# Cosformer attention and a two-of-eight expert layer in one kernel: attention in sub-chunks of 64 tokens, every attention product in four 64x64 tiles of TensorE's array

## The chip, the cores and the metric

The kernel runs on one core of one Trainium2 chip. The metric is the time of one execution on the device in microseconds (us). TensorE (PE) multiplies matrices, VectorE (DVE), ScalarE (ACT) and GpSimd (POOL) work elementwise, SyncE (SP) issues DMAs. Matrix products land in PSUM, in the program the array `ps` of eight banks of 512 floats on 128 partitions; everything else lies in SBUF. A matmul holds one operand in the array (LDWEIGHTS loads it) and streams the other through. Every matmul that the program writes on 32-bit floats appears in the trace as two loads and two matmuls; transposes, and matmuls of the type F32R, appear as one.

## What is computed

`x` has 2,048 tokens of 128 features. The first half is attention with 16 heads of 64 features on the normalised tokens (weights and biases as arrays):

```python
Q, K, V = (xn @ Wq + bq), (xn @ Wk + bk), (xn @ Wv + bv)      # 16 heads of 64
Qp, Kp = relu(Q), relu(K)
# at each token t, with cos_t and sin_t of the angle pi/(2T) * t:
S_cos += (Kp*cos_t) outer V;  S_sin += (Kp*sin_t) outer V     # 64x64 per head
z_cos += Kp*cos_t;            z_sin += Kp*sin_t
num = (Qp*cos_t) @ S_cos + (Qp*sin_t) @ S_sin
den = max(sum(Qp*cos_t*z_cos + Qp*sin_t*z_sin), 1e-6)
x = x + concat_heads(num / den) @ Wo + bo
```

The state runs over all tokens, so the attention is causal. The second half normalises again, picks the best 2 of 8 experts for each token, and adds `gelu(x @ w1 + b1) @ w2 + b2` of both, weighted by the softmax of their two scores.

## The kernel before

**Stages.** The tokens go through four stages `i` of 512 (NS = 4), each of four chunks `c` of 128 (SC = 4). A stage has a *front* (projections to qT, kT, kn and vcs, with the tail of the stage before between them) and an *attention* part. After the last stage come 39 expert blocks of 128 rows (`hidden`, `down`), which read rows that were scattered to `ybuf` by expert.

**A chunk of attention.** Queries and keys lie transposed in qT and kT (a head on 64 partitions, two heads to a slot), keys also by token in kn, and values times cos and times sin, with a column for z, in vcs (65 columns each, VW). The denominator needs no separate product: it is that column. The work of a stage is 16 groups `n` of four heads (four groups to a chunk), taken in 8 pairs `p`:

- `scores` (L1135): keys by queries for eight heads, 128x128 each, into banks 0 and 1. VectorE multiplies them by `pair` (1 + tan tan, causal) into `am` (`masked`, L751).
- `before` (L1152): queries by the state up to this chunk, 130 columns (cos and sin side by side), 64 partitions deep.
- `within` (L1173): `am` by the chunk's values, 65 columns, added to the cos half in PSUM, and then keys by values (L1180), 130 columns, into a third region of the same banks: what the chunk adds to the state.
- ScalarE copies the sine half out (`out_sums`, L598), VectorE adds the third region to `state` (L761) and joins the halves, cos + tan * sin, into `tcs` (L767). Banks 2 to 5 are two pairs that the groups take in turn.
- Once a chunk, VectorE makes the reciprocals (L771, L774), GpSimd scales (`normalise`, L432, into `on`, which has two buffers), TensorE turns the result in eight transposes (`turn_out`, L1200), ScalarE copies it to `oT` (L553), and TensorE projects it (`project`, L1209). VectorE adds the projection to `x_sb` (`residual`, L779).

**Sizes and tiles of the array.** L1135 and L1152 run as two matmuls at a time in two halves of the rows (64x128), L1173 and L1180 in two halves of the columns (128x64), all others in the whole array.

**Order.** Each engine's instructions stand in an order written out by hand, with a wait on a semaphore wherever one engine needs another. TensorE's order in attention is, for p = 1 to 8: scores(p), outputs(p-1), then a turn or a projection. Beside that, in stages 1 to 3, VectorE ranks the tokens of the stage before (`places` L854 to L864, after masked(1)), ScalarE takes the tanh for their shares (`share`, after group 1), VectorE writes the shares (`shares` L845, after groups 0 and 1), and GpSimd sends the rows to `ybuf` in eight scattered DMAs (`rows_paced`, L474), spread over the stage by the groups that are done. GpSimd also adds the bias bo (`open_residual`, L440) and normalises the next stage's x (L446). SP may load the first two expert blocks only when the last of stage 2's rows has landed (L384, L377), and TensorE turns both (L1259) at the end of attention 3, in `first_rows`.

Of the kernel before, what the change touches and what calls it, by code (L numbers as in the profile page):

```python
# [28 lines left out]
P = 128  # L29
# [12 lines left out]
CS = 2 * VW  # L42
GH = 4
# [8 lines left out]
PH = 2 * GH  # L52
PAIRS = GROUPS // 2
# [6 lines left out]
OT_AT, WO_AT, YT_AT, GATE_AT = 3, 5, 11, 14  # L60

# [30 lines left out]

def z_bank(b):

    return 7 if b >= Z_TWO and b % 2 else 4
# [5 lines left out]
def moe_block(nc, x, Wq, bq, Wk, bk, Wv, bv, Wo, bo, gate_w, w1, b1, w2, b2,  # L101
              c_rot, c_pair, c_ident, c_small, c_tri, c_ids, out, ybuf, zbuf):
    with ExitStack() as ctx:
# [19 lines left out]
        pair = sb("pair", [P, SC, P])  # L123
# [5 lines left out]
        blank = sb("blank", [P, BR, ROW])  # L129
# [10 lines left out]
        am = sb("am", [P, 2, 2, PH // 2, P])  # L140
        state = sb("state", [P, NP, CS])
# [3 lines left out]
        on = sb("on", [P, 2, H, DH])  # L145
# [21 lines left out]
        slot = sb("slot", [P, 2, SC], U32)  # L167
# [8 lines left out]
        w1b = [sb(f"w1b{k}", [P, F]) for k in range(2)]  # L176
# [5 lines left out]
        xb = sb("xb", [P, XR, P])  # L182
# [15 lines left out]
        os = sb_attn("os", [P, 2, 2, 2 * CS])  # L198
        vb = os[:].rearrange("p a r n -> p (a r n)")[:, 0:HD].rearrange("p (a n) -> p a n", a=2)
# [56 lines left out]
        os_ok = sem("os_ok")  # L256
        tcs_ok = sem("tcs_ok")
        st_ok = sem("st_ok")
# [60 lines left out]
        def _(sp):  # L319
# [17 lines left out]
            sp.dma_start(on[:, 1, 0:4, :], c_tri.rearrange("p s (h d) -> p (s h) d", d=DH)).then_inc(tri_in, 16)  # L337
# [5 lines left out]
            def pair_in_next(i, c):  # L343
                sp.wait_ge(am_ok, i * PAIRS + (c + 1) * 2)
                sp.dma_start(pair[:, c, :], c_pair[:, (i + 1) * SC + c, :]).then_inc(pair_in[c], 16)

            def blank_next(e):

                sp.dma_start(ybuf[e * PITCH:e * PITCH + T, :].rearrange("(p s) w -> p (s w)", p=P),
                             blank[:].rearrange("p s w -> p (s w)")).then_inc(blank_out, 16)  # L350
# [59 lines left out]
        def _(pool):  # L410
# [10 lines left out]
            pool.memset(blank[:], 0.0).then_inc(memsets, 1)  # L421
# [5 lines left out]
            def normalise(i, c):  # L427

                pool.wait_ge(rden_ok, i * SC + c + 1)
                if c >= 2:  # L430
                    pool.wait_ge(oT_ps, i * 2 * SC + 2 * (c - 1))
                pool.tensor_tensor(on[:, c % 2, :, :], tcs[:, c % 2, :, 0:DH],  # L432
                                   rden[:, c % 2, :, None].broadcast_to([P, H, DH]), ALU.mult
                                   ).then_inc(on_ok, 1)

# [28 lines left out]
            def rows_out(u, m):  # L464
# [9 lines left out]
                pool.indirect_dma_start(ybuf, bass.IndirectOffsetOnAxis(ap=slot[:, k, c:c + 1], axis=0),  # L474
# [9 lines left out]
            def attention(i):  # L484
                if i >= 1:
                    root(i - 1)
                    second_rows(i - 1)
                for c in range(SC):
                    if i >= 1 and c < 2:
                        pool.wait_ge(oT_ps, (i - 1) * 2 * SC + 2 * (c + SC - 1))  # L490
                    if i == 0 and c == 1:
                        pool.wait_ge(tri_ok, 1)
# [4 lines left out]
                    if i >= 1:  # L497
                        rows_paced(i, c)
                    normalise(i, c)
# [6 lines left out]
                    if i == NS - 1 and c == 2:  # L506
                        root(NS - 1)
# [7 lines left out]
            for i in range(NS):  # L515
                attention(i)
            second_rows(NS - 1)
# [15 lines left out]
        def _(act):  # L533
# [14 lines left out]

            def turn_out(i, c):

                for half in range(2):
                    act.wait_ge(oT_ps, i * 2 * SC + 2 * c + half + 1)
                    act.activation(oT[:, c % 2, half * 4:half * 4 + 4, :],  # L553
                                   ps[:, 6 + half, :].rearrange("p (a b) -> p a b", b=P), ACT.Copy
                                   ).then_inc(oT_ok, 1)
# [31 lines left out]
            def x_turned(i):  # L587
                act.wait_ge(xT_ps, i + 1)
                act.activation(xT_hi[:], ps[:, 6, :], ACT.Copy).then_inc(xThi_ok, 1)

            def out_sums(i, n):

                act.wait_ge(o_ps, i * GROUPS + n + 1)
                if n == 0:
# [868 lines left out]
```

## Time and profile before

| | |
|---|---|
| runs | 376.83 us median of 3 (376.57 to 377.76) |
| the profiled execution | 377.03 us, its span 375.2 us |
| mean granted clock of TensorE | 0.985 |
| TensorE matmul, weight load | busy 94%, 85% of the span |
| VectorE, ScalarE, GpSimd | busy 65%, 42%, 35% |
| fronts 1, 2, 3 | about 26 us each |
| attention 0, 1, 2, 3 | 38.2, 40.2, 40.2, 42.5 us |
| expert blocks and the end | 103 us |

Busy time of an engine is the union of its instructions. TensorE's matmuls overlap (each is shown for 0.22 to 0.28 us, though another may start 0.1 us or less behind it), so what a group of them costs is read from the start of its first to the start of the next group. The times that a timeline row gives are start and length; the bracket is how long the engine was idle before it and who ended that.

### The profile page before, as it was taken

Reading aid. Unit: us, or ns where it says so; the run is one execution under the profiler, and the core shown is the slowest. Engines: PE = TensorE matmul, PEld = TensorE weight load, DVE = VectorE, ACT = ScalarE, POOL = GpSimd, SP = SyncE. Lnnn points to the kernel's source line nnn. Section 1 sums busy time; section 2 is a strip of 40 time slices with the busy share of each in tenths; the row PEclk is TensorE's granted clock in tenths of the full one; section 3 lists DMA queues with packets and bytes.
Section 4 is the critical chain, followed back from the end, with each engine's and each line's share of the span. In section 5 each row is a group of like instructions: output and inputs, shape, how many; then the busy total and the mean of one; then the engine's idle time right before and its main releaser. Section 6 shows DMA issues by size and latency. Waiting matters only on the chain.

```text
span 375.2 us, 10993 instructions
## 1 busy us (share of the span) xinstructions
PE 351.7 (94%) x4125; PEld 319.0 (85%) x4125; DVE 244.9 (65%) x774; ACT 156.5 (42%) x369; POOL 130.1 (35%) x130
## 2 busy tenths in 40 slices
PE   7999999999999999999999999999899999999920
PEld 7877999888899988889898888999789899999910
DVE  4889665768966566896646679866656554444515
ACT  4773231467222146622214672212345555555510
POOL 4022522212086320207732030455037675444530
PEclk9999999999999999999999999999999999999985
DMA  7941530531001000000100005300646677667129
GB/s 254 309 206 40 229 136 10 210 128 52 9 24 48 18 2 1 0 9 27 41 17 9 3 0 145 98 27 26 171 126 191 186 206 213 187 192 192 35 60 282
DMA packets 32773, 38.65 MB, mean 103 GB/s; under 512 B 4140, under 2 KB 25025, under 8 KB 31697
## 3 DMA queue, kind: packets, MB, share of 16 engines
q1 hardware_dynamic: 27248, 31.90, 27.5%
q0 software_dynamic: 2272, 4.46, 3.5%
q10 hardware_dynamic: 3200, 1.58, 1.4%
q8 instruction: 34, 0.56, 0.6%
q14 instruction: 19, 0.15, 0.1%
HBM read 22.91 MB, written 15.47 MB: 102 GB/s over the span
## 4 chain that ended last, share of the span: by engine, by line
PE 82%; DVE 5%; DMA 5%; issue 3%; POOL 1%; ACT 1%; SPq 1%; ACTq 0%; DVEq 0%; POOLq 0%
PE ps L1135 9%; PE ps L1173 9%; PE ps L1359 8%; PE ps L1344 8%; PE ps L1152 7%; PE ps L1180 7%; PE ps L1209 7%; PE ps L1054 6%; PE ps L1056 5%; PE ps L1055 5%; PE ps L1200 4%; PE ps L1099 3%; DMA zin<-zbuf 2%; PE ps L1331 1%; DMA ident<-c_ident 1%
## 5 line engine op out<-in xcount | busy, mean ns | idle before, releaser
L598 ACT ACTIVATE os<-ps 128x260 f32<-128x260 f32 x64 | 24.9, 389 | 99.8 <-PE ps L1180 99.8
L639 ACT ACTIVATE hT<-ps,b1t 128x128 f32<-128x128 f32 x156 | 44.6, 369 | 38.6 <-PE ps L1344 38.6
L474 POOL DMA_INDIRECT ybuf<-yr,slot x32 | 31.9, 997 | 69.4 <-DVE yr L846 31.7
L432 POOL TENSOR_TENSOR on<-tcs,rden 128x1024 f32<-128x1024 f32 x16 | 30.4, 1903 | 65.0 <-DVE rden L774 65.0
L512 POOL DMA_INDIRECT zbuf<-z,tokens x39 | 38.0, 975 | 31.1 <-DVE z L997 25.6
L761 DVE TENSOR_TENSOR state<-ps,state 128x260 f32<-128x260 f32 x64 | 27.4, 428 | 32.4 <-ACT os L598 30.1
L751 DVE TENSOR_TENSOR am<-ps,pair 128x1024 f32<-128x1024 f32 x32 | 38.7, 1208 | 9.3 <-issue 6.7
L1359 PE MATMUL ps<-w_sb,hT 128*128 x312 | 43.1, 281 | 0.6 <-DVE zs L993 0.4
L1344 PE MATMUL ps<-xb,w1b 128*128 128x128 f32 x312 | 42.3, 278 | 0.0
L1173 PE MATMUL ps<-vcs,am 128*64 128x65 f32 x1024 | 42.2, 225 | 0.0
L1173 PEld LDWEIGHTS ps<-vcs,am 128*64 128x64 f32 x1024 | 36.8, 137 | 3.9
L1180 PE MATMUL ps<-vcs,kn 128*64 128x130 f32 x512 | 39.5, 275 | 0.0
L1359 PEld LDWEIGHTS ps<-w_sb,hT 128*128 128x128 f32 x312 | 37.8, 191 | 1.9 <-issue 1.4
L1135 PE MATMUL ps<-qT,kT 64*128 64x128 f32 x512 | 37.2, 284 | 1.0 <-DVE am L751 0.9
L1344 PEld LDWEIGHTS ps<-xb,w1b 128*128 128x128 f32 x312 | 37.9, 192 | 0.0
L1135 PEld LDWEIGHTS ps<-qT,kT 64*128 64x128 f32 x512 | 31.2, 187 | 6.9 <-issue 6.2
L716 DVE TENSOR_SCALAR vcs<-os,cs 128x512 f32<-128x512 f32 x64 | 32.6, 552 | 1.1
L1152 PE MATMUL ps<-state,qT 64*128 64x130 f32 x480 | 33.3, 277 | 0.0
L1209 PE MATMUL ps<-wo_sb,oT 128*128 128x128 f32 x256 | 31.6, 278 | 0.0
L712 DVE TENSOR_TENSOR os<-ps,bv_all 128x512 f32<-128x512 f32 x32 | 22.0, 689 | 14.6 <-PE ps L1056 14.6
L1209 PEld LDWEIGHTS ps<-wo_sb,oT 128*128 128x128 f32 x256 | 29.8, 192 | 1.7 <-issue 1.4
L1152 PEld LDWEIGHTS ps<-state,qT 64*128 64x128 f32 x480 | 30.2, 187 | 0.8 <-issue 0.7
(121 smaller groups left out, 590.0 us busy)
## 6 DMA issues: line engine op xcount, KB each, us to landing
w1b<-in_L_ffn_w SPq DMA_DIRECT2D x39, 256.0 KB, 2.9
ybuf<-blank SPq DMA_DIRECT2D x8, 1152.0 KB, 4.6
yb<-ybuf SPq DMA_DIRECT2D x39, 72.0 KB, 2.9
w_sb<-in_L_ffn_w SPq DMA_DIRECT2D x8, 256.0 KB
x_sb<-in_L_attn_x SPq DMA_DIRECT2D x4, 256.0 KB, 5.2
pair<-c_pair SPq DMA_DIRECT2D x16, 64.0 KB, 2.3
zin<-zbuf SPq DMA_DIRECT2D x4, 256.0 KB, 4.8
zin<-zbuf ACTq DMA_DIRECT2D x4, 256.0 KB, 5.3
```

The lines of the kernel that those rows point to most:

```text
L474: pool.indirect_dma_start(ybuf, bass.IndirectOffsetOnAxis(ap=slot[:, k, c:c + 1], axis=0), yr[:, k, c, :], None).then_inc(y_out[u], 16)
L512: pool.indirect_dma_start(zbuf, bass.IndirectOffsetOnAxis(ap=tokens[:, b:b + 1], axis=0), z[:, b % ZR, :], None, bounds_check=2 * T - 1, o ...
L639: act.activation(hT[:, b % 2, f, :], ps[:, b % 2 * 2 + f // 2, f % 2 * P:f % 2 * P + P], ACT.Gelu, bias=b1t[:, b % XR, f:f + 1]).then_inc( ...
L716: last = dve.tensor_scalar(vcs[:, m // 2, (m % 2) * 8:(m % 2) * 8 + 8, s, 0:DH], vb[:, m % 2, :].rearrange("p (h d) -> p h d", d=DH), cs4[ ...
L751: dve.tensor_tensor(am[:, p % 2, :, :, :], ps[:, 0:2, :].rearrange("p r (q t) -> p r q t", t=P), pair[:, c, None, None, :].broadcast_to([P ...
L1135: last = mm(ps[:, r, b * P:(b + 1) * P], kT[rows, of, c * P:(c + 1) * P], qT[rows, of, c * P:(c + 1) * P], start=True, stop=True)
L1152: mm(ps[:, 2 + 2 * (n % 2) + r, 0:2 * CS].rearrange("p (s b v) -> p b s v", s=2, b=2)[:, q, :, :], qT[rows, 2 * g + q, c * P:(c + 1) * P], ...
L1173: mm(ps[t:t + 64, 2 + 2 * (n % 2) + r, q * VW:q * VW + VW], am[:, n // 2 % 2, r, (2 * g + q) % (PH // 2), t:t + 64], vcs[:, c, g * GH + 2 ...
L1180: last = mm(ps[64 * r:64 * r + 64, 2 + 2 * (n % 2) + q, 2 * CS:3 * CS], kn[:, c, (2 * g + q) * P + r * DH:(2 * g + q) * P + (r + 1) * DH], ...
L1209: last = mm(ps[:, 7, at:at + D], oT[:, c % 2, pr, :], wo_sb[:, pr, :], start=(pr == 0), stop=(pr == NP - 1))
L1344: last = mm(ps[:, b % 2 * 2 + f // 2, f % 2 * P:f % 2 * P + P], w1b[b % WR][:, f * P:(f + 1) * P], xb[:, b % XR, :], start=True, stop=True ...
L1359: last = mm(ps[:, z_bank(b), 0:D], hT[:, b % 2, f, :], w, start=(f == 0), stop=(f == FB - 1))
```

## The change

Attention is cut into sub-chunks of 64 tokens inside the chunk of 128, and every product of it uses 64x64 tiles, in rounds of four (rows halves by column halves).

- `scores(n)` makes only the two diagonal 64x64 blocks of each head: 8 program matmuls a group, moving 64 columns. `masked` multiplies 128x512 elements instead of 128x1024.
- `key_values(n)` makes keys by values for each half of the chunk apart: 8 program matmuls, 130 columns, one bank for each half of tokens.
- VectorE makes from that two sums: `half_state` (the state after the first 64 tokens, into `mid`) and `whole_state` (after all 128, into the other of two `state` buffers), each 128x260 elements, the second waiting for the first.
- `from_state(n, a)` multiplies the 64 queries of sub-chunk a by `state` (a = 0) or `mid` (a = 1): 16 program matmuls a group, 65 columns. The sine part takes queries times tan (`qtan`), so cos and sine add up in PSUM. GpSimd makes `qtan` in 8 products of 128x512 a stage (`sine_queries`).
- `within(n, cross)` multiplies `am` by the values: 8 program matmuls of 65 columns a group in two calls of four; the second waits for the first on TensorE's own semaphore.
- ScalarE copies the finished sums to `tcs` (`sums_out`, 128x260); `out_sums`, the buffer `os` and L767 are gone. The group's region in PSUM is used twice: for keys by values, and, when VectorE has read that, for the sums. Three pairs of banks (2 to 7) take turns.
- A turned chunk is now 16 transposes of 64 rows: chunks 0 and 1 in two parts of eight (`turn_part`) between groups, in the spare halves of banks 0 and 1; chunks 2 and 3 in one. `on` has one buffer.
- The projections of chunks 0 and 1 come after the groups, that of chunk 2 moves to the next front (in stage 3 behind the first `hidden`). `scores(0)` and `scores(1)` stand in the front.
- `places(i-1)` now comes before VectorE's work for group 0, `shares(i-1)` after masked(1), which follows group 1. The norm of the first two chunks of stage 3 and its routing move behind the attention part, between the expert blocks.
- `blank`, `xb` and two of the `w1b` buffers share one piece of SBUF; `Wo`'s rows and `c_pair` are laid out for the new order (96 KB a chunk instead of 64 KB).

The core of the diff, in the order of the kernel:

```diff
 # gpsimd
+            def sine_queries(i, c):
+                pool.wait_ge(pair_in[c], i * 16 + 16)
+                for half in range(2):
+                    pairs = slice(half * 4, half * 4 + 4)
+                    pool.wait_ge(big_ok, i * QK_JOBS + NP + half * 4 + 4)
+                    if c >= 2:
+                        pool.wait_ge(o_ps, i * GROUPS + (c - 2) * NG + half * 2 + 2)
+                    pool.tensor_tensor(qtan[:, c % 2, pairs, :], qT[:, pairs, c * P:(c + 1) * P],
+                                       pair[:, c, None, HT:TR].broadcast_to([P, 4, P]), ALU.mult).then_inc(qt_ok, 1)
...
+                sine_queries(i, 0)
+                sine_queries(i, 1)
                 for c in range(SC):
...
                     if i >= 1:
                         rows_paced(i, c)
+                    if c + 2 < SC:
+                        sine_queries(i, c + 2)
                     normalise(i, c)
 # vector
+            def half_state(i, n):
...
+                dve.wait_ge(kv_ps, i * GROUPS + n + 1)
...
+                dve.tensor_tensor(mid[:, n % 2, :, :], ps[:, slot(n), 0:2 * CS].rearrange("p (b v) -> p b v", b=2),
+                                  state[:, c % 2, 2 * g:2 * g + 2, :], ALU.add).then_inc(mid_ok, 1)
+            def whole_state(i, n):
...
+                dve.wait_ge(mid_ok, i * GROUPS + n + 1)
...
+                for n in range(GROUPS):
+                    if tail and n == 0:
+                        places(i - 1)
+                    if n >= NG + 1 and n % NG == 1:
+                        reciprocals(i, n // NG - 1)
...
+                    half_state(i, n)
+                    whole_state(i, n)
+                    if n % 2 == 1 and n // 2 + 1 < PAIRS:
+                        masked(i, n // 2 + 1)
+                    if tail and n == 1:
+                        shares(i - 1)
 # tensor
+            def from_state(i, n, a):
...
+                if a == 0:
+                    pe.wait_ge(st_ok, i * GROUPS + n + 1)
+                    pe.wait_ge(qt_ok, i * QT_JOBS + 2 * c + g // 2 + 1)
+                for s in range(2):
+                    for r, q in TILES:
...
+            def group(i, n):
+                if n < GROUPS:
+                    key_values(i, n)
+                if n >= 1:
+                    from_state(i, n - 1, 0)
+                    from_state(i, n - 1, 1)
+                    within(i, n - 1, 0)
+                if n + 2 < GROUPS:
+                    scores(i, n + 2)
+                if n >= 1:
+                    within(i, n - 1, 1)
...
+                for n in range(GROUPS + 1):
+                    group(i, n)
...
+                    if n in TURN_AT:
+                        turn_part(i, *TURN_AT[n])
```

`TURN_AT` is {8: (0, 0), 10: (0, 1), 12: (1, 0), 14: (1, 1)} (chunk, part).

## Rows read from the trace of the kernel before

**Rows 1.** The page of the profile, part 1: busy us of each engine, share, instructions.

```profile
PE 351.7 (94%) x4125; PEld 319.0 (85%) x4125; DVE 244.9 (65%) x774; ACT 156.5 (42%) x369; POOL 130.1 (35%) x130
```

**Rows 2.** Windows of attention 2 and attention 3: stretch, then each engine's busy us.

```profile
163.30:203.50 40.20, 40.19 (x701) 37.08 (x701) 26.25 (x58) 10.33 (x25) 16.82 (x15) 1.00 0.08 24
229.70:272.20 42.50, 41.42 (x706) 37.61 (x707) 30.22 (x80) 10.07 (x25) 14.32 (x12) 1.00 0.36 104
```

**Rows 3.** Timeline of TensorE, one pair of groups: start us, us, engine, line.

```profile
110.01 1.16 PE L1135 MATMUL ps<-qT,kT 64*128 64x128 f32 x16
111.00 1.06 PE L1152 MATMUL ps<-state,qT 64*128 64x130 f32 x16
112.00 0.69 PE L1173 MATMUL ps<-vcs,am 128*64 128x65 f32 x16
112.51 0.62 PE L1180 MATMUL ps<-vcs,kn 128*64 128x130 f32 x8
...
113.97 0.49 PE L1135 MATMUL ps<-qT,kT 64*128 64x128 f32 x4
```

**Rows 4.** Timeline of TensorE: matmuls that follow one another into one tile.

```profile
255.03 0.20 PE L1250 MATMUL ps<-match,small 128*1 128x17 f32 x2
255.08 0.20 PE L1252 MATMUL ps<-match,small 128*1 128x17 f32 x2
```

**Rows 5.** Waits of TensorE's queue, by source line, 32 to 33 us: min/median/max ns, start.

```profile
L1131 PEldq EVENT_SEMAPHORE  x1: 51/51/51, 32.5 to 32.5; - x1
...
L1168 PEldq EVENT_SEMAPHORE  x1: 51/51/51, 32.6 to 32.6; - x1
```

**Rows 6.** Timeline of TensorE: turning a chunk, and two projections.

```profile
184.44 1.09 PE L1200 MATMUL ps<-ident,on 128*128 128x128 f32 x8
185.46 1.16 PE L1135 MATMUL ps<-qT,kT 64*128 64x128 f32 x16
...
189.42 3.84 PE L1209 MATMUL ps<-wo_sb,oT 128*128 128x128 f32 x32
193.10 0.60 PE L1061 MATMUL ps<-ident,xh 128*128 128x128 f32 x4
```

**Rows 7.** Groups by line and shape, whole run: busy us, mean ns, idle before.

```profile
L432 POOL TENSOR_TENSOR on<-tcs,rden 128x1024 f32<-128x1024 f32 x16 | 30.4, 1903 | 65.0 <-DVE rden L774 65.0
...
L761 DVE TENSOR_TENSOR state<-ps,state 128x260 f32<-128x260 f32 x64 | 27.4, 428 | 32.4 <-ACT os L598 30.1
...
L598 ACT ACTIVATE os<-ps 128x260 f32<-128x260 f32 x64 | 24.9, 389 | 99.8 <-PE ps L1180 99.8
L712 DVE TENSOR_TENSOR os<-ps,bv_all 128x512 f32<-128x512 f32 x32 | 22.0, 689 | 14.6 <-PE ps L1056 14.6
...
L446 POOL TENSOR_SCALAR xh<-x_sb,mv,rstd 128x128 f32<-128x128 f32 x12 | 9.4, 789 | 0.0
...
L440 POOL TENSOR_TENSOR x_sb<-x_sb,bo_all 128x512 f32<-128x512 f32 x4 | 5.1, 1282 | 0.0
```

**Rows 8.** Timeline of VectorE around the start of attention 3.

```profile
232.09 0.18 DVE L854 TENSOR_TENSOR pos<-ps,cnt 128x32 f32<-128x32 f32 x1
...
232.64 0.22 DVE L864 TENSOR_REDUCE slot<-sel 128x8 uint32<-128x64 f32 x1
```

**Rows 9.** Timeline of GpSimd in attention 2.

```profile
169.60 1.08 POOL L474 DMA_INDIRECT ybuf<-yr,slot  x1 [15.03 <-DVE yr L846]
...
181.17 0.96 POOL L474 DMA_INDIRECT ybuf<-yr,slot  x1 [0.30 <-issue]
```

**Rows 10.** Timeline of GpSimd and VectorE where front 3 begins.

```profile
203.68 1.91 POOL L432 TENSOR_TENSOR on<-tcs,rden 128x1024 f32<-128x1024 f32 x1 [10.36 <-DVE rden L774]
...
203.98 1.63 DVE L692 COPY cs<-rot 128x16 f32<-128x16 f32 x1
```

**Rows 11.** Timeline of GpSimd and TensorE: the last rows out, then both blocks in.

```profile
258.61 0.96 POOL L474 DMA_INDIRECT ybuf<-yr,slot  x1 [3.02 <-DVE state L761]
...
266.73 0.33 PE L1259 MATMUL ps<-ident,yb 128*128 128x128 f32 x1 [0.83 <-DMA yb<-ybuf]
```

More of the change, by code:

```diff
@@ L175, in moe_block @@
         yb = [sb(f"yb{k}", [P, ROW]) for k in range(3)]
-        w1b = [sb(f"w1b{k}", [P, F]) for k in range(2)]
+        w1b = [spare[:, XR * P + k * F:XR * P + (k + 1) * F] for k in range(2)]
         b1_all = sb("b1_all", [P, E, FB])
@@ L1118, in front @@
                 scores(i, 0)
+                scores(i, 1)
                 values(V_JOBS - 1)
@@ new lines, in key_values @@
+                last.then_inc(kv_ps, 1)
+            def from_state(i, n, a):
+                c, g = n // NG, n % NG
+                if a == 0:
[3 more added lines that the diff above has]
+                    for r, q in TILES:
+                        rows, of, half = slice(HT * r, HT * r + HT), 2 * g + q, HT * (a ^ q)
+                        ask = (qT[rows, of, c * P + HT * a:c * P + HT * a + HT] if s == 0 else
+                               qtan[rows, c % 2, of, HT * a:HT * a + HT])
+                        held = state[rows, c % 2, of, :] if a == 0 else mid[rows, n % 2, q, :]
+                        mm(ps[half:half + HT, slot(n) + r, q * VW:q * VW + VW], ask, held[:, s * VW:s * VW + VW],
+                           start=(a == 0 and s == 0), stop=True, skip_group_check=True)
@@ new lines, in within @@
+            def within(i, n, cross):
+                c, g = n // NG, n % NG
+                if cross == 0:
+                    pe.wait_ge(am_ok, i * PAIRS + n // 2 + 1)
+                else:
+                    pe.wait_ge(own_ps, i * GROUPS + n + 1)
+                for a, q in ((0, 0), (1, 0), (0, 1), (1, 1)):
+                    r, rows, half = a ^ cross, slice(HT * a, HT * a + HT), HT * (a ^ q)
+                    last = mm(ps[half:half + HT, slot(n) + r, q * VW:q * VW + VW],
+                              am[rows, n // 2 % 2, r, (2 * g + q) % (PH // 2), :], vcs[rows, c, g * GH + 2 * r + q, 0, :],
+                              start=False, stop=True, skip_group_check=True)
+                last.then_inc(o_ps if cross else own_ps, 1)
@@ new lines, in group, with turn @@
+            def group(i, n):
[9 more added lines that the diff above has]
+                    within(i, n - 1, 1)
+            def turn(i, c, part, bank, at):
+                for pr in range(4 * part, 4 * part + 4):
+                    for k in range(2):
+                        rows = slice(HT * k, HT * k + HT)
+                        last = pe.transpose(ps[:, bank + k, at + pr % 4 * HT:at + pr % 4 * HT + HT],
+                                            on[rows, 2 * pr:2 * pr + 2, :].rearrange("p h d -> p (h d)"),
+                                            ident[rows, rows])
+                last.then_inc(oT_ps, 1)
```

452 lines of the change are left out of this document (206 added, 246 removed).

## The prediction

> **What bounds the kernel now.** I read the page first: TensorE is busy 94% of the span, VectorE 65%, GpSimd 35% [rows 1]. An average hides the stages, so next the windows: in attention 2, TensorE is busy 40.19 of 40.20 us, VectorE 26, ScalarE 10, GpSimd 17 [rows 2]. Nobody makes TensorE wait there, so a matmul saved is time saved, as long as the others follow. Then the timeline of one pair of groups, for the price of each product by the distance of the starts [rows 3]: scores 1.00 us, state products 1.00, within 0.51, keys by values 0.45; a pair takes 3.97 here, and 4.03 with the small waits in others. A stage has 8 pairs, 32.2 us; stage 0 has no state product in two of them, 30.2.
>
> **The price of a round.** Sixteen instructions of 128 columns in two tiles take 1.00, so two side by side cost 0.112 us after the first; sixteen of within (64 columns loaded, 65 streamed) take 0.51, two side by side 0.058 (14 x 0.058/2 and the first, which pays some 0.05 for the change of tile shape); eight of 130 columns take 0.45, two side by side 0.112 [rows 3]. Row halves and column halves each double the work of a round at no cost. No row shows both at once. I take the same round for four tiles: 0.058 and 0.112 us. Lower bound: the same, since what is streamed in each tile is no shorter. Upper bound: each matmul for itself at 0.025 us, the distance of the starts of two followers in one tile (0.05 for two [rows 4]), 0.100 for four. I take the lower, because TensorE's queue can feed it: between its wait at L1131 (32.5 us) and the one at L1168 (32.6) stand all 32 instructions of a scores call [rows 5], so four loads and four matmuls come in far less than 0.058 us.
>
> Here the Trainium skill speaks against the change: "TensorE: Matmul & The Clock Gate", in the section on the 56 ns of a matmul, says that starts never come closer than about 25 ns however small the matmul is. The trace agrees within one tile (0.025). By that rule a round of four would be 0.100 us; that case is the rival B.
>
> **Removed and added on TensorE.** A stage of the new kernel has, in rounds of four instructions, 64 of scores, 128 from the state, 64 within (0.058 each, 14.8 us) and 64 of keys by values (0.112, 7.2 us): 22.0 us, 1.38 a group. Work saved: 32.2 - 22.0 = 10.2 us in three stages, 8.2 in stage 0, **38.8 us** in all. The diagonal blocks save it (half of scores and within); the rest has as many columns as before.
>
> **What is given back.**
> - The second call of within waits for the first, with four rounds of scores (0.23 us) between and a matmul shown for 0.22 to 0.27. I take 0.07 a group, from 0 to 0.15: 1.1 a stage, **4.5**.
> - Turns. A chunk costs 1.02 now [rows 6]. A part is 8 transposes, two side by side at best (0.45), and two changes of shape at 0.15: 0.75. Four parts and two whole turns of 1.1 are 5.2 against 4.1 a stage: **4.4** (2 to 8, if they don't go side by side).
> - The new loop. A group's keys by values must be added twice by VectorE before the state products may write the same region: 0.27 for the last matmul to land, 0.43 twice (as L761 [rows 7]) and 0.03 between them, 1.16 us. TensorE has 0.93 us of other work after that product and then the next one (0.45): covered, with 0.2 to spare. VectorE's own load a group: 0.81 for the two sums (a follower starts 0.08 before the end), half of a 128x512 product (0.69 as L712 [rows 7], spaced 0.61), 1.1 against 1.38. It is covered in the steady state only.
> - Where the cover is gone: the reciprocals stand before group 5, 9 and 13 and cost 0.5 us while a group's sums wait, of which 0.25 gets through, three a stage, and 0.3 at the end of a stage: **4.2** in all.
> - The start of attention. VectorE still ends the last values 0.7 us in and in stages 1 to 3 does places (232.09 to 232.86, 0.75 us [rows 8]) before group 0: the state products start 2.4 us in instead of 1.1, later if a vector instruction stands behind GpSimd's new products. I take 2.0 lost in three stages, 0.7 in stage 0: **6.7** (3 to 11).
> - shares. VectorE now waits, after masked(1), for ScalarE's tanh, which stands behind the copy of group 1. Behind that wait is half_state(2), for which TensorE waits. From the end of group 1's products: 0.27, 0.39 (L598 [rows 7]), 0.2 for the tanh, 0.15, and then 0.9 for the sums, 2.0; less 0.45 for keys by values, which TensorE does meanwhile: **1.5** a stage, 4.5.
> - GpSimd. It gets 8 products of 128x512 a stage, 1.28 each as L440 [rows 7], 10.3 us to 17 [rows 2]; 27 of 40, but in a fixed order. From the start of attention 1 or 2 (163.30): the first row starts at 6.3 (169.60), two rows take 2.5 (0.96 and 0.30 of idle each [rows 9]), two sine products 2.6, chunk 0's normalise 1.9 (L432 [rows 7]), four of xh 3.1 (L446 [rows 7]), three rows 3.8, two sine products 2.6, chunk 1's normalise 1.9: done at 24.7. TensorE ends group 0's products at about 3.8 (2.4 to 3.2 for the start, 1.0 of work) and asks for the turn 12 rounds of its loop on, less one: 3.8 + 11 x 1.45 + 1.5 for shares + 1.5 for two parts = 22.8. Late by about **1.9** in two stages, 3.8. In stage 0 there are no rows, in 3 no xh.
> - Stage 3. The table's instructions between groups 2 and 7 hold VectorE 0.9. first_rows needs the second block, which lands 8.1 us after the last row's scatter starts (258.61 to 266.73 [rows 11]). By GpSimd's order that start is 27.2 us in: chunk 2's sums are there at 25.2 (22.8, 0.9 of table, two parts), its normalise takes 1.9. So the block is in at 35.3. TensorE comes at 31.4 (3.8 + 15 x 1.45 - 1.15 for calls that the last groups lack + 1.05 + 1.5 + 0.9 + 3.0 of parts + 0.5). It waits 3.9 instead of 0.8: with the table **4.0**.
> - Behind attention 3 the norm and routing of its first half now stand between expert blocks: turn_y waits some 0.7 us for yr, **1.0**. The pair's larger DMAs (96 KB) have a whole stage's time: nothing; without that, 1 us. The expert blocks keep their instructions; the shared buffer is written again only after its zeros are out, long before: nothing.
>
> Sum: 38.8 - (4.5 + 4.4 + 4.2 + 6.7 + 4.5 + 3.8 + 4.0 + 1.0) = 38.8 - 33.1 = 5.7, and from the profiled execution (span 375.2, 377.03 in all) 371.3. That execution is 0.2 above the median of the runs, so **371.1 us**.
>
> Another lock is in sight: a 128x16 copy of VectorE that starts inside a GpSimd product took 1.63 us and ended with it [rows 10]. "SBUF — State Buffer" in the Trainium skill, where it reads its diagram, says that the port pair shared by both is locked for a whole instruction, also against a VectorE instruction with two SBUF inputs. The new maximum in reciprocals has two. By the rule it would wait up to 1.9 us, 12 times, some 5 us more, 376; I keep it in the range only, as the sums and masks read PSUM and one SBUF input (L761 keeps 0.43 beside GpSimd).
>
> **Rivals.**
> A, the losses overlap. A TensorE that is late at the start asks later for everything, and each queue may be ahead of my chain by a microsecond. Then only the turns, the own wait and half of the starts count: 38.8 - 4.4 - 4.5 - 5 = 25, **352 us** (346 to 362, by how much of each overlaps). For it: 40.19 us of work and engines at 26 and 17 of 40. Against: the waits for places, shares and normalise are written in order, and each is counted on an instruction's length.
> B, a round of four costs more than one of two. At 0.100 instead of 0.058 each of 1,024 short rounds loses 0.042, 43 us, and nothing on the long ones: 371 + 43, less some 18 of the losses, which a slower TensorE hides: **396 us**. It decides from 0.064 on, where 1,024 x 0.0056 is my whole gain. For it: no row has four tiles, and followers at 0.025. Against: rows 5 and starts that lie side by side in both shapes.
> C, GpSimd sets the pace. With 1.9 us for each sine product (strided queries; L432's price for twice the elements) the order above ends 2.5 us later by group 12 and 5 by the last row: stages 1 to 3 lose 2.5, 2.5 and 4: **380 us**.
> D, the tiles don't run as four because the compiled matmul is something else: as B.
>
> **How the numbers follow.** A measurement here tells about 0.3%, 1.1 us, from no change. My case, 362 to 375: 0.45. A, below 362: 0.25. C and my case with the lock or longer waits, 375 to 385: 0.15, a half of it within 0.3%. B and D: 0.15. So faster 0.70, same 0.07, slower 0.23. The range leaves out B and D and the best 0.03 of A: 348 to 384. The forecast is the first case's time.
>
> **What would show it.** Right: rounds of four with starts 0.058 apart; VectorE's sums at 0.43; TensorE idle in every stage at the first from_state, after group 1 for the sums, in stages 1 and 2 at the third or fourth part of a turn for GpSimd; L1259's counterpart waiting for its block some 4 us; GpSimd busy 40 us more. Attention about 34, 39, 39 us. Wrong: a round well above 0.06 (B), an idle of TensorE below 2 us a stage (A), sine products far from 1.28 (C).

## The result, and the profile after

The changed kernel takes 419.93 us (419.11 to 422.48, four runs) against 376.70 (376.25 to 377.76): ratio 1.1144, 95% interval 1.1101 to 1.1186. The forecast of 371.1 has the wrong sign, and 419.9 lies outside the range of 348 to 384. The profiled execution took 422.48, its span 420.7. Of the runs below, the last has three executions of ten that lie over 1.5% above its fastest, and its ratio leaves them out.

The page of the changed kernel: part 1, the row of TensorE's clock, the queue that brings the instructions, the chain that ended last.

```profile
PE 346.9 (82%) x6845; PEld 310.9 (74%) x6845; DVE 239.2 (57%) x773; ACT 158.0 (38%) x385; POOL 171.5 (41%) x162
...
PEclk9996998999979999996999999689999999999985
...
q8 instruction: 55, 0.90, 0.9%
...
PE 67%; DVE 15%; issue 9%; DMA 4%; ACT 2%; POOL 2%; SPq 1%; ACTq 0%; DVEq 0%; POOLq 0%
```

TensorE was busy 94% [rows 1]; now 82%, with 6,845 matmuls for 4,125 (and 55 packets of instructions for 34), and "issue" is 9% of the chain: time in which it waited for nothing that the profile shows. The windows of the four attention stages, then of attention 1 and 3 before (TensorE, its loads, VectorE, ScalarE, GpSimd, granted clock, DMA share, GB/s):

```profile
32.20:77.30 45.10, 32.19 (x1281) 29.30 (x1280) 24.76 (x50) 9.35 (x25) 19.27 (x15) 0.89 0.30 117
112.50:153.30 40.80, 30.93 (x1281) 27.74 (x1280) 22.70 (x54) 8.52 (x24) 22.43 (x20) 0.92 0.10 29
188.40:229.30 40.90, 31.61 (x1282) 28.28 (x1281) 22.45 (x54) 8.39 (x24) 22.37 (x20) 0.92 0.10 28
264.60:305.50 40.90, 33.04 (x1287) 29.92 (x1287) 25.76 (x62) 8.51 (x24) 19.08 (x16) 0.88 0.22 61
```

```profile
98.90:135.30 36.40, 36.40 (x654) 33.39 (x652) 22.63 (x51) 9.78 (x23) 16.95 (x15) 1.00 0.08 26
...
231.60:270.20 38.60, 37.52 (x660) 33.85 (x657) 26.53 (x72) 9.56 (x23) 14.32 (x12) 1.00 0.32 92
```

The stages were to shrink and grew, to 167.7 us in all. The windows of before sum to 146.7 (35.3, 36.4, 36.4 and 38.6), but they begin behind the second pair's scores and the first product from the state (1.0 us each), whose counterparts the windows of the changed kernel have in them. Begun at those scores (32.57, 96.95, 163.30 and 229.67) they are 36.4, 38.4, 38.4 and 40.6, 153.7 in all: the stages grew by 14 us, though two projections (3.84 [rows 6]) have left each. TensorE is idle in them for 10 us of 41 and 13 of 45, no other engine fills the gap, and the clock is no longer 1.00. The fronts between grew from 28.0 to 35.2 us (the two projections now stand behind the loop, and there is a new wait of 2.7), the part behind attention 3 from 105.0 to 115.2.

The timeline of TensorE in attention 1 shows what became of [rows 3]: first a group that nothing holds up, then two places a few us on.

```profile
123.31 0.30 PE L1217 MATMUL ps<-state,qT 64*64 64x65 f32 x8
123.43 0.30 PE L1217 MATMUL ps<-state,qtan 64*64 64x65 f32 x8
...
123.78 0.30 PE L1229 MATMUL ps<-vcs,am 64*64 64x65 f32 x8
123.89 0.42 PE L1176 MATMUL ps<-qT,kT 64*64 64x64 f32 x16
124.27 0.34 PE L1229 MATMUL ps<-vcs,am 64*64 64x65 f32 x8
124.43 0.63 PE L1199 MATMUL ps<-vcs,kn 64*64 64x130 f32 x16
124.88 0.29 PE L1217 MATMUL ps<-state,qT 64*64 64x65 f32 x8
...
125.34 0.28 PE L1229 MATMUL ps<-vcs,am 64*64 64x65 f32 x2
126.62 0.28 PE L1229 MATMUL ps<-vcs,am 64*64 64x65 f32 x3 [1.00 <-issue]
...
132.36 0.30 PE L1176 MATMUL ps<-qT,kT 64*64 64x64 f32 x8
134.16 0.29 PE L1176 MATMUL ps<-qT,kT 64*64 64x64 f32 x5 [1.50 <-issue]
...
134.56 0.46 PE L1252 MATMUL ps<-ident,on 64*128 64x64 f32 x8
```

Eight matmuls in 0.115 to 0.12: a round of four is 0.058 us, and of 130 columns 0.112 (16 in 0.45), exactly the forecast; the group takes 1.57 us (123.31 to 124.88). The prediction had 1.38, and 0.07 for the wait of the second call of within for the first (TensorE's own wait), which here is 0.15. A part of a turn costs 0.39 (the next call starts at 134.95) where 0.75 was put. Then the engine stops in the middle of a call, for no semaphore. Counting matmuls from stop to stop gives 126 to 128 each time, that is 252 to 256 instructions with the loads: the stops at 125.4, 129.6, 132.4, 137.0, 140.5, 144.9 and 148.8 are 1.2, 0.7, 1.7, 0.9, 1.4, 1.3 and 1.35 us long. The queue "instruction" brings 16 KB at a time; from 123.8 us to the end of this stage its packets start 3.6 to 4.3 us apart and take 0.9 to 1.6 us. A stage asks for ten such blocks, 37 to 40 us at 3.7 to 4.0 each, and took 40.8. In all four stages these stops come to some 32 us (11.0, 8.5, 8.5, 4.0).

The rest is at the start of the stages. Timeline of attention 1's start, three engines:

```profile
108.04 3.72 POOL L462 TENSOR_TENSOR qtan<-qT,pair 128x512 f32<-128x512 f32 x3 [5.44 <-ACT qT L609]
...
108.20 1.15 DVE L867 CAST idxf<-idx 128x8 f32<-128x8 uint32 x1
109.38 1.24 DVE L872 TENSOR_TENSOR hot<-small,idxf 128x64 f32<-128x64 f32 x1
110.66 1.15 DVE L876 TENSOR_TENSOR any<-hot 128x32 fp32r<-128x32 f32 x1
...
111.86 0.28 PE L1299 MATMUL ps<-any,tri 128*128 128x32 f32 x1 [2.66 <-DVE any L876]
...
115.46 0.50 PE L1217 MATMUL ps<-state,qT 64*64 64x65 f32 x8 [1.60 <-DVE state L799]
115.74 0.44 PE L1217 MATMUL ps<-state,qtan 64*64 64x65 f32 x8
...
121.73 0.34 PE L1217 MATMUL ps<-state,qT 64*64 64x65 f32 x8 [0.80 <-DVE state L799]
```

Three VectorE instructions, 0.17, 0.23 and 0.19 in the kernel before (means of the groups of idxf, hot and any), each last as long as one product of GpSimd, and TensorE waits 2.7 us for them. Then come the foreseen wait for the state (1.9 us between the starts) and shares (1.2). Behind these idles eight matmuls take 0.22 instead of 0.12: TensorE is at 1.2 GHz (granted clock 0.50 in 115.4 to 118.0 and in 118.0 to 120.9), 2 to 2.5 us lost. Stages 0, 2 and 3 have the same stretch, and two shorter ones of 3.4 us begin at the end of the longest stop of stage 0 (66.7) and of the wait for `match` in stage 3 (280.8), some 3 us more. In stage 3 two more instructions meet GpSimd (same view):

```profile
276.66 1.69 DVE L805 TENSOR_TENSOR dmax<-tcs,cs 128x16 f32<-128x16 f32 x1 [0.53 <-ACT tcs L636]
278.72 1.91 POOL L450 TENSOR_TENSOR on<-tcs,rden 128x1024 f32<-128x1024 f32 x1 [0.41 <-DVE rden L809]
278.78 1.88 DVE L927 SCALAR_TENSOR_TENSOR match<-small,ps,ex 128x17 f32<-128x17 f32 x1
280.81 0.40 PE L1176 MATMUL ps<-qT,kT 64*64 64x64 f32 x12 [2.79 <-DVE match L927]
```

### The profile page after: what moved, and what is told of

The parts are those of the page before. It is cut to its first block, busy times and chain, and to the rows that moved or that the text cites. A ratio compares the mean times of both kernels' runs of the same rounds, so it can differ in the third digit from the quotient of the medians.

```text
span 420.7 us, 16544 instructions
## 1 busy us (share of the span) xinstructions
PE 346.9 (82%) x6845; PEld 310.9 (74%) x6845; DVE 239.2 (57%) x773; ACT 158.0 (38%) x385; POOL 171.5 (41%) x162
## 4 chain that ended last, share of the span: by engine, by line
PE 67%; DVE 15%; issue 9%; DMA 4%; ACT 2%; POOL 2%; SPq 1%; ACTq 0%; DVEq 0%; POOLq 0%
PE ps L1217 8%; PE ps L1403 7%; PE ps L1388 7%; PE ps L1275 7%; PE ps L1199 6%; PE ps L1229 5%; PE ps L1079 5%; PE ps L1081 4%; PE ps L1080 4%; PE ps L1176 3%; PE ps L1252 2%; DVE vcs L745 2%; PE ps L1126 2%; DVE vb L741 2%; DMA zin<-zbuf 2%
## 5 line engine op out<-in xcount | busy, mean ns | idle before, releaser
L462 POOL TENSOR_TENSOR qtan<-qT,pair 128x512 f32<-128x512 f32 x32 | 40.6, 1289 | 29.9 <-ACT qT L609 19.9
L1199 PE MATMUL ps<-vcs,kn 64*64 64x130 f32 x1024 | 48.6, 303 | 3.2 <-issue 3.0
L1229 PE MATMUL ps<-vcs,am 64*64 64x65 f32 x1024 | 45.9, 242 | 6.2 <-issue 5.2
L503 POOL DMA_INDIRECT ybuf<-yr,place x32 | 31.8, 993 | 35.0 <-DVE state L799 26.7
L793 DVE TENSOR_TENSOR mid<-ps,state 128x260 f32<-128x260 f32 x64 | 26.9, 420 | 29.4 <-PE ps L1199 28.7
L1229 PEld LDWEIGHTS ps<-vcs,am 64*64 64x64 f32 x1024 | 31.7, 146 | 8.7 <-issue 5.7
L1176 PE MATMUL ps<-qT,kT 64*64 64x64 f32 x1024 | 30.9, 234 | 8.6 <-issue 5.5
L1199 PEld LDWEIGHTS ps<-vcs,kn 64*64 64x64 f32 x1024 | 33.0, 150 | 5.8 <-issue 4.4
L1176 PEld LDWEIGHTS ps<-qT,kT 64*64 64x64 f32 x1024 | 25.1, 148 | 11.0 <-issue 11.0
L745 DVE TENSOR_SCALAR vcs<-vb,cs 128x512 f32<-128x512 f32 x64 | 31.3, 532 | 1.1
L1275 PE MATMUL ps<-wo_sb,oT 128*128 128x128 f32 x256 | 30.7, 276 | 0.1
```

Source lines behind the costliest of these rows:

```text
L462: pool.tensor_tensor(qtan[:, c % 2, pairs, :], qT[:, pairs, c * P:(c + 1) * P], pair[:, c, None, HT:TR].broadcast_to([P, 4, P]), ALU.mult) ...
L503: pool.indirect_dma_start(ybuf, bass.IndirectOffsetOnAxis(ap=place[:, k, c:c + 1], axis=0), yr[:, k, c, :], None).then_inc(y_out[u], 16)
L745: last = dve.tensor_scalar(vcs[:, m // 2, (m % 2) * 8:(m % 2) * 8 + 8, s, 0:DH], vb[:, m % 2, :].rearrange("p (h d) -> p h d", d=DH), cs4[ ...
L1176: last = mm(ps[HT * a:HT * a + HT, r, at:at + HT], kT[rows, of, here], qT[rows, of, here], start=True, stop=True, skip_group_check=True)
L1199: last = mm(ps[HT * r:HT * r + HT, slot(n) + a, q * CS:q * CS + CS], kn[rows, c, (2 * g + q) * P + r * DH:(2 * g + q) * P + (r + 1) * DH], ...
L1229: last = mm(ps[half:half + HT, slot(n) + r, q * VW:q * VW + VW], am[rows, n // 2 % 2, r, (2 * g + q) % (PH // 2), :], vcs[rows, c, g * GH ...
```

## The experiments

Three theories. **1, the supply:** TensorE's instructions arrive at 256 in some 3.7 us, and four small tiles ask for them faster. **2, the array or the banks** stop. **3, the lock and the order:** GpSimd's new products hold VectorE up, and the waits that follow idle TensorE and its clock. Times are medians; the ratio is to the kernel before on the same chip, with its interval.

| run | us | ratio | attention stages, us |
|---|---|---|---|
| changed kernel | 419.9 | 1.114 (1.110 to 1.119) | 45.1, 40.8, 40.9, 40.9 |
| no tangent products | 399.6 | 1.061 (1.057 to 1.065) | 39.4, 36.9, 37.4, 40.0 |
| merged | 408.5 | 1.086 (1.079 to 1.094) | 40.9, 35.2, 35.4, 37.0 |
| both | 383.8 | 1.021 (1.018 to 1.024) | 37.6, 31.9, 33.2, 34.2 |
| wider | 424.1 | 1.129 (1.122 to 1.136) | 41.1, 38.6, 41.5, 42.8 |
| order | 409.8 | 1.087 (1.081 to 1.093) | 43.9, 38.2, 40.4, 42.5 |
| products added to before | 402.4 | 1.067 (1.062 to 1.073) | not read |
| complete, merged | 382.2 | 1.019 (1.013 to 1.026) | 34.9, 30.3, 30.7, 36.6 |
| and last stage | 373.4 | 0.990 (0.987 to 0.994) | 35.0, 31.1, 31.6, 31.4 |

**TensorE alone.** A kernel of stretches of this loop, each behind 24 products of 512 columns:

```
for k in range(count):
    r, a = TILES[k % 4]
    rows, half = slice(HT * r, HT * r + HT), slice(HT * a, HT * a + HT)
    mm(ps[half, 2 + r + 2 * (k // 4 % 2), 0:cols], data[rows, 64 * (k // 4 % 4):64 * (k // 4 % 4) + HT],
       data[rows, 512:512 + cols], start=True, stop=True, skip_group_check=True)
```

> Nothing of the layer is computed: TensorE alone runs six stretches, each behind 24 products of 128x128 by 512 columns. Four 64x64 tiles in turn, fp32, 65 columns (256 products, that is 512 loads and 512 matmuls); two column tiles of 128x64, 65 columns; four tiles at 130 and at 260 columns; four tiles in bf16 at 65 columns (512 products, 512 loads and 512 matmuls); the first stretch again while 16 MB of transfers run. Theory 1, the supply of instructions: the first stretch begins at 14.5 ns a matmul and then stops at every 256 instructions, so that 128 matmuls take about 3.7 us (29 ns each); the bf16 stretch takes the same 3.7 us per 128 matmuls though its columns pass faster; the two-tile stretch and the 130-column one, whose array time for 128 matmuls is 3.6 to 3.7 us, are at the edge and show small stops; the 260-column one shows none (about 7 us for 128). With the transfers running the stops are longer, or as long if they do not share a path. Theory 2, the stops in the changed kernel come from the array or the banks: the first stretch goes on at 14.5 ns, 1.86 us for 128 matmuls, with no stops at 256 instructions.

The windows of the six stretches, in the order of the text (TensorE, its loads, ScalarE, GpSimd, granted clock, DMA share, GB/s; the fifth is bf16, the last has transfers running), then the timeline of the first, the bf16 and the last:

```profile
31.70:44.50 12.80, 8.18 (x512) 7.76 (x512) 0.00 (x0) 0.00 (x0) 1.00 0.02 5
65.50:80.40 14.90, 14.90 (x513) 14.90 (x512) 0.00 (x0) 0.00 (x0) 1.00 0.01 3
101.30:115.50 14.20, 14.20 (x513) 14.17 (x512) 0.00 (x0) 0.00 (x0) 1.00 0.02 5
136.50:164.40 27.90, 27.90 (x513) 19.46 (x512) 0.00 (x0) 0.00 (x0) 1.00 0.01 2
185.50:197.50 12.00, 5.70 (x513) 5.34 (x512) 0.00 (x0) 0.00 (x0) 0.74 0.02 4
220.30:240.80 20.50, 12.33 (x513) 11.77 (x512) 0.00 (x0) 0.00 (x0) 0.71 0.94 263
```

```profile
31.70 2.79 PE L61 MATMUL ps<-x_sb 64*64 64x65 f32 x175
35.56 2.09 PE L61 MATMUL ps<-x_sb 64*64 64x65 f32 x128 [1.08 <-issue]
39.57 2.09 PE L61 MATMUL ps<-x_sb 64*64 64x65 f32 x128 [1.91 <-issue]
43.29 1.43 PE L61 MATMUL ps<-x_sb 64*64 64x65 f32 x81 [1.64 <-issue]
...
190.00 1.25 PE L61 MATMUL ps<-low 64*64 64x65 bf16 x128 [2.34 <-issue]
193.73 1.98 PE L61 MATMUL ps<-low 64*64 64x65 bf16 x128 [2.48 <-issue]
...
226.36 3.74 PE L61 MATMUL ps<-x_sb 64*64 64x65 f32 x128 [2.99 <-issue]
232.01 3.74 PE L61 MATMUL ps<-x_sb 64*64 64x65 f32 x128 [1.91 <-issue]
```

No other engine works here, and the stop comes at exactly every 128 matmuls, 256 instructions. The first 175, which stand behind slow products, run at some 14.5 ns each; from then on a block of 256 takes 3.7 to 4.0 us, and in bf16 3.7 and 3.5 (190.00 to 193.73 to 197.18), though 128 bf16 matmuls, once they are there, pass in about 1.1 at the full clock. Two tiles (3.73 us for 128 matmuls) and 130 columns (3.55) have no stop, where small ones were expected: their own time covers the fetch, which so needs no more than 3.55 where nothing has stopped. With 263 GB/s of transfers beside it a block takes 5.7 to 7.0 us: 3.7 of work at 1.2 GHz and then a stop of 1.9 or 3.3. The packets of the instruction queue start at the same distances: 3.5 to 3.9 us in the first stretch, 3.4 to 3.8 in the one of 130 columns, 5.8 and 7.0 in the last. Theory 2 falls for the stops, 1 holds with its number.

**No tangent products.**

```
-                sine_queries(i, 0)
-                sine_queries(i, 1)
...
-                        ask = (qT[...] if s == 0 else qtan[rows, c % 2, of, ...])
+                        ask = qT[...]
```

> GpSimd's products of queries with the tangent are left out, and TensorE's sine half takes the unscaled queries in their place: the same instructions on TensorE, no product on GpSimd. Theory 3, the lock of GpSimd's products on VectorE and the waits they cause: the first product from the state comes 3 us earlier in stage 0, VectorE's chain to the ranks is 2.7 us shorter in each of the other three, the waits of 1.9, 1.6 and 0.8 us at the start of attention go, and the stretches at 1.2 GHz behind them (about 2 us each) go: 12 to 20 us faster, 400 to 408 us. Theory 1, the supply of instructions bounds the stages: the stops at every 256 instructions stay, and as they begin earlier, a part of the gain is given back: 6 to 12 us faster, 408 to 414 us. That the products are hidden: no change, 420 us.

20.3 us faster, a little beyond the upper end of theory 3. The wait for the ranks is gone (front 1 takes 32.3 us for 35.2), the granted clock of attention 1 and 2 is 1.00 though the waits at the first product from the state (1.8) and behind group 1 (1.5) stayed, against the expectation: they are made by VectorE's own order, not by the products. The stops at 256 instructions stayed as well (6.7 us in attention 1 and 7.5 in 2 where there were 8.5).

**Merged.**

```
-                for s in range(2):
+                for s in range(1):
...
-                        mm(ps[half:half + HT, slot(n) + r, q * VW:q * VW + VW], ask, held[:, s * VW:s * VW + VW],
+                        mm(ps[half:half + HT, slot(n) + r, q * CS:q * CS + CS], ask, held,
```

> The product from the state streams both halves, 130 columns, from one load of the queries in place of 65 columns twice (the sine half of the result is left out): per group 16 of 80 matmuls and 16 loads fewer, the same columns. Theory 1, the supply of instructions, 14.4 ns each where it bounds: 0.46 us a group less, 7 us a stage, 24 to 30 us in all: 390 to 396 us. Theory 2, the array: the same columns, the same time, 416 to 420 us. Theory 3, the waits for other engines: 416 to 420 us too.

The stages lose 19 us (148.5 for 167.7) with the same columns, so theory 2 falls again, and the stops at 256 instructions fall from 32 us to some 11 (1.7 and 2.1 in attention 1 and 2); the total only 11.5 (the profiled executions differ by 14), as the part behind attention 3 grew by 5 us, with waits of 1.7 and 3.2 for the first two blocks' rows where there was one of 0.8: TensorE is early. The size expected, 24 to 30, was too large: it took every removed instruction at the fetch's price, but a stretch is held by the fetch only where the fetch exceeds its work and its other waits.

**Both edits.**

> The tangent products are left out (as in the run without them) and the product from the state is merged (as in the run with 16 matmuls fewer a group; the sine half of the result is left out). If the lock and the supply are two causes that add up, 20 and 11.5 us: 388 us (385 to 391). If they hide one another (an earlier start only runs into the next stop for instructions), 395 to 400 us. With 64 matmuls a group, 128 instructions by 14.4 ns are 1.84 us against 1.5 to 1.6 of products: the stops at 256 instructions stay, at half their size or less.

383.8: the two causes do not hide one another. Together the edits give 36.1 us, one by one 31.8, so 388 (385 to 391) was expected and they gave 4 more; what the 4 are was not looked for.

**Wider.** Same instructions, more columns.

```
+                        mm(ps[half:half + HT, slot(n) + r, q * CS:q * CS + (CS if s == 0 else VW)], ask, held if s == 0 else held[:, VW:CS],
```

> The same instructions, but the cosine half of the product from the state streams 130 columns in place of 65 (the added columns land beside the sums and are not read): 0.22 us more of the array per group at the rounds' prices (0.112 for 0.058 us, four rounds), 3.5 us a stage. Theory 2, the array sets the pace: 12 to 14 us slower, 432 to 434 us. Theory 1, the supply of instructions does: no change or up to 4 us slower, 420 to 424 us.

424.1 (420.5 to 427.9): 4 to 5 us more than the changed kernel (the intervals of the ratios, 1.122 to 1.136 and 1.110 to 1.119, lie just apart), at the upper end of theory 1's 420 to 424 and not 12 to 14. In the profiled execution, the fastest of the four (span 418.7 for 420.7), the stages take 164.0 us for 167.7 though they move more columns: the stops of attention 1 sum to 4.3 us where they were 8.5. Columns fill the time of the fetch; this is what supply means.

**Order.**

```
+                if i >= 1:
+                    pool.wait_ge(any_ok, i)
                 sine_queries(i, 0)
...
                     whole_state(i, n)
+                    if tail and n == 0:
+                        places(i - 1)
```

> Nothing is left out; three things change their place in the order. GpSimd begins the tangent products of a stage only when VectorE has its routing masks (any) ready, places stands behind the second sum of group 0 and shares behind group 3. Theory 3, the order and the lock cost: TensorE's wait of 2.7 to 2.9 us for the ranks goes in three stages, the 1.9, 1.6 and 0.8 us at the first product from the state shrink to about 0.5, the waits of 1.2 to 1.5 us after group 1 go, and with them the stretches at 1.2 GHz: 405 to 410 us. Theory 1, the supply of instructions bounds the stages and takes back what comes behind the wait: only the 8 us of the ranks: 411 to 413 us. That none of this matters: 420 us.

10.1 us faster, at the edge between the two sums. The ranks' wait is gone (attention 1 starts at 108.25 for 112.51) and that for shares too; the wait at the first product from the state did not shrink to 0.5 but grew (2.17 for 1.86): the tangent products now start later and fall beside the last two scalings of the values (L747, 1.89 us for the two, where the same two took 0.88 without products), which stand ahead of the state's first sum. And theory 1's give-back is to be seen: in attention 3 the stops at 256 instructions sum to 11.6 us where they were 4.0, probably because the waits of 1.5 and 3.0 us in which the fetch caught up are gone.

**The products added to the kernel before.**

```
+                    pool.tensor_tensor(qtan[:], qT[:, pairs, c * P:(c + 1) * P],
+                                       pair[:, c, None, :].broadcast_to([P, 4, P]), ALU.mult).then_inc(qt_ok, 1)
```

> The kernel before with GpSimd's tangent products added at the places that they have in the changed kernel; nobody reads them, nothing else changes, and TensorE's instructions are the old ones. Theory 3, the lock and GpSimd's time are a cost of their own: VectorE's chain to the ranks is late by 2 to 3 us in three stages and stage 0's last values by 1 to 2, and the rows and normalised sums on GpSimd later by some us: 6 to 14 us slower, 383 to 391 us. Theory 1 alone: within 2 us of before.

26.6 us slower, where 6 to 14 were expected. Waits of TensorE in its attention 1 and before it, by the timeline:

```profile
99.20 0.28 PE L1250 MATMUL ps<-any,tri 128*128 128x32 f32 x1 [1.19 <-DVE any L856]
...
116.23 1.16 PE L1218 MATMUL ps<-ident,on 128*128 128x128 f32 x8 [2.27 <-POOL on L435]
128.71 0.44 PE L1218 MATMUL ps<-ident,on 128*128 128x128 f32 x2 [1.82 <-POOL on L435]
```

The largest part is not the lock but GpSimd's order: the normalised sums stand behind two products and the rows, and the turns wait for them. That was this prediction's term "GpSimd late", 4.1 us here in attention 1 where it had 1.9; five such waits sum to 10.3 us of idle, the three for the ranks to 3.6. Behind three of the former and two of the latter TensorE is at 1.2 GHz for 3.4 us each, which accounts for some of the rest. The changed kernel has no wait for the normalised sums, since it is late itself. So the cost of the products is 20 us in one kernel and 26 in the other, but by different waits.

**The lock by itself.** VectorE runs six kinds, four of each, alone and beside GpSimd.

> Nothing of the layer is computed: VectorE runs six kinds of instructions, four times each (PSUM plus SBUF 128x260; a copy of 128x16 in SBUF; the larger of two SBUF inputs, 128x16; a scaled copy of 128x512 in SBUF; the sum of two SBUF inputs, 128x512; a copy of 128x512 from PSUM), first alone, then beside GpSimd's products of two SBUF inputs of 128x512, one behind the other, then beside GpSimd's scaled copies with one input. Theory 3: alone 0.1 to 0.7 us each. Beside the products, instructions that only touch SBUF take up to the 1.28 us of a product, as max and idxf did, and those that read PSUM keep their times (0.43 for 260 columns). Beside the copies with one input nothing changes, or as much if every GpSimd instruction locks. If the long instructions of the traces waited for data instead: no change anywhere.

The timeline, four instructions a row: alone, then beside products of two SBUF inputs.

```profile
9.34 0.80 DVE L79 COPY a<-x_sb 128x16 f32<-128x16 f32 x4
...
11.01 1.81 DVE L83 TENSOR_SCALAR c<-x_sb 128x512 f32<-128x512 f32 x4
```

```profile
20.27 1.82 DVE L77 TENSOR_TENSOR e<-ps,x_sb 128x260 f32<-128x260 f32 x4 [1.45 <-POOL pool_out L57]
22.12 2.40 DVE L79 COPY a<-x_sb 128x16 f32<-128x16 f32 x4
...
27.28 5.58 DVE L83 TENSOR_SCALAR c<-x_sb 128x512 f32<-128x512 f32 x4
```

PSUM and SBUF together: 0.43 each, as alone. A copy within SBUF: 0.17 alone, up to 1.12 beside; 512 columns 0.43 alone and 1.37 beside, the sum of two SBUF inputs 0.69 and 1.63. Beside GpSimd's copies with one input small copies took 0.17 to 0.46, those of 512 columns 0.68 to 0.84 and the sums 0.69 to 1.08: a lock too, but a short one, between the two cases expected. Beside the products it is as expected.

**A complete kernel of these tiles.** Merged, no product on GpSimd, the tangent on the sums, places behind group 0, shares behind group 3:

```
+                for q in range(2):
+                    last = act.activation(os[:, n % 2, :, q * VW:q * VW + VW],
+                                          ps[:, slot(n):slot(n) + 2, q * CS + VW:q * CS + CS],
+                                          ACT.Copy, scale=cs4[:, 4 + q, c:c + 1])
...
+                dve.tensor_tensor(tcs[...], ps[:, slot(n):slot(n) + 2, 0:2 * CS][...], os[...], ALU.add)
```

> A complete kernel of the same 64-token tiles: the product from the state is merged (64 matmuls a group), no tangent product on GpSimd; ScalarE scales the sine half of the sums by the tangent of the token (two of 128x130 a group), VectorE adds it (a third sum a group), places stands behind group 0 and shares behind group 3. By the supply, 1.84 us a group, and the lock gone, it is the time of the run with both edits less 2 to 4 us for the order, plus 0 to 6 us for VectorE, which then has 1.6 of the 1.84 us a group: 383 to 392 us. If the fetches are hidden by the other waits: 378 to 383 us. VectorE as the new bound (a group at 2.0 us or more): 392 to 400 us.

382.2, just below the 383 to 392 expected and in the range for fetches hidden by other waits (378 to 383), with stages 1 and 2 of 30 to 31 us that nearly run through (stops of 0.7 and 0.8 us): VectorE's third sum fits in. Its last stage takes 36.6 and shows the lock once more; the run after it moves that instruction:

```profile
237.17 1.88 DVE L933 SCALAR_TENSOR_TENSOR match<-small,ps,ex 128x17 f32<-128x17 f32 x1
```

```
+                    if i == NS - 1 and n == 5:
+                        match_blocks(0)
                     if n >= 2:
                         combined(i, n - 2)
...
-                for m, groups in ROWS_AT:
+                for m, groups in ROWS_AT if i < NS - 1 else ROWS_LAST:
```

> The complete merged kernel with two places changed in the last stage: VectorE matches the first table's blocks ahead of the sums and reciprocals of its turn, so that this does not fall beside GpSimd's normalised sums (it took 1.88 us there, and TensorE waited 2.5), and GpSimd sends all rows of stage 2 ahead of chunk 1's sums. Theory 3, the lock and the order: the match takes about 0.25 us, TensorE's wait falls from 2.5 to below 1, the wait for the second block (1.8 us) goes: 2 to 4 us faster than the complete merged kernel, 378 to 380 us (its profiled span 377.7 to about 374.5). If neither decides: 382 us.

```profile
237.00 0.23 DVE L934 SCALAR_TENSOR_TENSOR match<-small,ps,ex 128x17 f32<-128x17 f32 x1
```

The match takes 0.23, the last stage 31.4, the whole 373.4 (370.8 to 378.1): 8.8 faster than the version without the two moves, where 2 to 4 were expected. The two were measured on different chips; their profiled executions differ by 6.5 (span 371.2 for 377.7), of which the last stage has 5.2. The two moves were not tried one by one. Against the kernel before the ratio says 1.0% faster (0.6 to 1.3) and the medians of all executions 0.7% (373.4 for 376.1), with ranges that overlap: with these tiles the kernel about breaks even, at most 1.3% ahead.

## Why the prediction was wrong

**The step that failed is "I take the lower, because TensorE's queue can feed it".** The price of a round was right, 0.058 and 0.112 us. But [rows 5] showed 32 instructions that already stood in the queue; that is a burst. A group asks for 160 instructions in 1.38 us, and TensorE alone shows 256 in about 3.7 us, so 160 take 2.3 (attention 1 took 2.55 a group, its other waits included). Over the length of a block nothing in attention before ran faster than 80 instructions a group of 2.0 us, and so no row showed the limit; the ends of the bound should have been an unlimited supply and what that trace shows to be sustained, 40 instructions a us. By that end a group takes 4.0 us, twice the old one; the truth lies between. Rival B priced a slow round from a follower in one tile (0.025), which four tiles don't pay: 14.5 ns a matmul was measured. It gave the right sign, 396, for a cause that isn't there. The stops sum to 32 us.

The Trainium skill, "Runtime: NRT & Kernel Launch", in the section on instruction fetch, says that instructions come in 16 KiB blocks of 256 and that crossing a block is mostly hidden. The block is what the trace shows; hidden it is here only while 256 instructions last at least 3.55 us.

**The lock was seen and not priced.** The text kept 5 us for the maximum in reciprocals (its mean is 0.63 for 0.25: 16 instructions, 6 us of VectorE, and in stage 3 one of 1.69 on the path). The chain to the ranks, all in SBUF and due when the new products start, was not in the sum at all: 2.7 to 2.9 us in three stages, 8.5; in stage 0 two scalings of the values (L745, 2.82 for the two) delay the first product from the state (a gap of 3.2 us, 1.3 without the products); the match of stage 3 2.8. "SBUF — State Buffer" in the Trainium skill has the rule (a port pair locked for a whole instruction), and the trace agrees: 1.15, 1.24, 1.15 beside products of 1.24.

**The clock was not in the sum.** It was 1.00 in every stage before. Behind the idles of 2.7 and 1.9 us TensorE worked at 1.2 GHz for some 5 us, 2 to 2.5 us lost a stage, about 9, and some 3 more in the two shorter stretches.

**Terms that held:** the start of attention (1.9, 1.6 and 0.8 us lost, 2.0 put), shares (1.2 to 1.5 for 1.5), the price of a tangent product (mean 1.29 for 1.28). Turns were cheaper (0.39 a part for 0.75), the own wait dearer (0.15 a group for 0.07). GpSimd was not late for the turns, and the wait for the second block was 0.5 for 3.9: TensorE came later than all of them.

Against the sum, which put the span 5.7 below before: 32 (supply), 8.5 and some 2.5 and 2.8 (lock), 12 (clock), 5 (own wait) make 63, less what the sum had and the trace did not: 3 for the second block, 5 for the turns, 4 for GpSimd, and most of the 4 for the reciprocals. That leaves some 48, and the span is 45.5 + 5.7 = 51.2 above it. The sizes are read off gaps between starts and partly overlap, so the fit is no proof; the two edits together take 36 us of it away.

## What to carry to other kernels

Halving the columns of small matmuls helps only down to where 256 of TensorE's instructions (a load and a matmul, twice for fp32) last as long as their fetch, about 3.5 to 3.7 us here: count instructions per us beside columns. A product moved to GpSimd is not free for being off the path: list the instructions of VectorE that fall beside it and read only SBUF or two operands there (`match` has a third in PSUM and took 1.88), and what stands behind it in GpSimd's own order. And where an engine has been idle, read the granted clock before pricing what follows.

## What was not expected of the hardware

The fetch of instructions is slower beside other transfers: 5.7 us and more for a block of 256 at 263 GB/s, 3.7 to 4.0 alone. It isn't the packet that grows (1.1 to 1.2 us there, 1.0 to 1.3 alone) but the time between two packets; what fills it no run shows. In the changed kernel, stage 0 has the longest stops (2.6 and 3.0 us), each behind a stretch of 259 GB/s. GpSimd's products gave way too: 1.26 us beside VectorE's instructions that read PSUM and 1.59 beside its sums of two SBUF inputs. And once the queue was empty, a bf16 matmul in four tiles of 65 columns came hardly sooner than an fp32 one (3.5 to 3.7 us for 128, and 3.7 to 4.0), though the first 239 of them had started 8 ns apart.
